# Layernorm, block quantisation and weight loads of an attention and FFN kernel moved to other chunks of a round

## The reference, cut to what matters

```python
xn = layernorm(x)                        # x: 4 sequences x 1024 tokens x 256, over the last axis
q, k, v = split(xn @ w_qkv.T)            # 16 heads of 128; rotary embedding on q and k
attn = softmax(q @ k.T / sqrt(128)) @ v
a = attn @ w_out.T
up_q, down_q = mxfp4(up_kernel), mxfp4(down_kernel)   # blocks of 32: power-of-2 scale, 8-value grid
f = gelu(xn @ up_q + up_bias) @ down_q + down_bias
out = x + a + f
```

## Time and profile before

| | before |
|---|---|
| median of 3 runs | 2655.05 us (2653.35 to 2657.96) |
| the profiled execution | 2657.86 us |
| its span, first to last instruction | 2656.1 us |
| PE busy | 2497.0 us, 94% |
| DVE busy | 2038.3 us, 77% |
| POOL busy | 1826.7 us, 69% |
| ACT busy | 1357.1 us, 51% |
| mean granted TensorE clock | 0.97 |

### The profile page before, as it was taken

How to read it: one execution, slowest core, us unless ns; L and a number is a source line. 1 busy time by engine, 2 the same in 40 slices (tenths; PEclk the granted TensorE clock), 3 DMA queues, 4 the chain that set the end, 5 groups by cost and what they waited for, 6 DMA issues and landing times. The chain is left out here.

```text
span 2656.1 us, 41956 instructions
## 1 busy us (share of the span) xinstructions
PE 2497.0 (94%) x12656; PEld 2166.2 (82%) x12656; DVE 2038.3 (77%) x3209; ACT 1357.1 (51%) x2518; POOL 1826.7 (69%) x1480
## 2 busy tenths in 40 slices
PE   6898999989899898989989898998989899898999
PEld 5787887878788787878878787887878788787788
DVE  6878778687777868787786877878687787868777
ACT  5455554545555454555545455554545555454333
POOL 5678776767777676777767677776768777676321
PEclk8999999999999999999999999999999999999999
DMA  3454545546554554546545454555655455454742
GB/s 100 124 141 115 142 121 129 135 119 171 147 138 124 128 134 121 135 119 171 152 127 135 126 133 116 142 126 132 160 154 129 119 141 129 119 133 114 207 164 64
DMA packets 233732, 354.30 MB, mean 133 GB/s; under 512 B 37840, under 2 KB 95440, under 8 KB 233424
## 3 DMA queue, kind: packets, MB, share of 16 engines
q1 hardware_dynamic: 233680, 353.72, 51.5%
HBM read 66.26 MB, written 18.87 MB: 32 GB/s over the span
## 5 line engine op out<-in xcount | busy, mean ns | idle before, releaser
L915 PE MATMUL o_ps<-keys_first,v_rows 128*128 128x256 f32 x4096 | 946.8, 385 | 4.1 <-DMA keys_first<-turned_blocks 4.1
L589 ACT ACTIVATE probs<-s_ps,neg_max 128x1024 f32<-128x1024 f32 x512 | 571.1, 1115 | 659.9 <-DVE neg_max L688 654.9
L688 DVE TENSOR_REDUCE neg_max<-s_ps 128x1 f32<-128x1024 f32 x512 | 622.2, 1220 | 363.8 <-PE s_ps L915 363.6
L915 PEld LDWEIGHTS o_ps<-keys_first,v_rows 128*128 128x128 f32 x4096 | 779.7, 194 | 109.2 <-DMA keys_first<-turned_blocks 4.5
L915 PE MATMUL s_ps<-seq_parts 128*128 128x512 f32 x3072 | 833.5, 409 | 11.1 <-ACT probs L589 7.1
L466 POOL TENSOR_TENSOR rope_a<-rope_a,cos 128x512 f32<-128x512 f32 x253 | 326.8, 1292 | 611.7 <-ACT rope_b L581 611.5
L915 PEld LDWEIGHTS s_ps<-seq_parts 128*128 128x128 f32 x3072 | 579.0, 189 | 130.5 <-ACT probs L589 7.3
L698 DVE STREAM_TRANSPOSE turned_blocks<-probs 128x512 f32<-128x512 f32 x1024 | 638.2, 679 | 33.3 <-ACT probs L589 14.8
L915 PE MATMUL slot_ps<-seq_parts,w_parts 128*128 128x512 f32 x1500 | 385.8, 392 | 0.0
L595 ACT ACTIVATE o_hi<-o_ps 128x256 fp32r<-128x256 f32 x256 | 98.6, 385 | 535.4 <-PE o_ps L915 535.4
L469 POOL TENSOR_TENSOR seq_parts<-rope_a,rope_b 128x512 fp32r<-128x512 f32 x253 | 327.0, 1293 | 19.8
(11 more groups left out here) (103 smaller groups left out, 2212.9 us busy)
## 6 DMA issues: line engine op xcount, KB each, us to landing
keys_first<-turned_blocks SPq DMA_DIRECT2D x2048, 128.0 KB, 2.7
w_raw<-in_w_qkv SPq DMA_DIRECT2D x96, 256.0 KB, 3.1
seq_parts<-xnt_parts SPq DMA_DIRECT2D x14, 1024.0 KB, 7.6
wo_raw<-in_w_out SPq DMA_DIRECT2D x64, 128.0 KB, 2.5
y<-in_x SPq DMA_DIRECT2D x16, 256.0 KB, 3.2
ln_x<-in_x SPq DMA_DIRECT2D x16, 256.0 KB, 3.5
xnt_parts<-ln_hi SPq DMA_DIRECT2D x16, 256.0 KB, 2.9
xnt_parts<-ln_lo SPq DMA_DIRECT2D x16, 256.0 KB, 3.3
```

The lines of the kernel that those rows point to most:

```text
L589: nc.scalar.activation(probs[:, k2 % 4, :], s_ps[k2 % 2][:, :], ACT.Exp, bias=neg_max[:, col:col + 1], accum_out=row_sum[:, col:col + 1]). ...
L688: nc.vector.tensor_reduce(neg_max[:, k2 % 16:k2 % 16 + 1], s_ps[k2 % 2][:, :], AXX, ALU.max, negate=True).then_inc(max_ready, 1)
L915: ins = nc.tensor.matmul(out, w, m, start=(n == 0), stop=(n == len(terms) - 1))
```

## The change

What a round adds is placed in other steps. `mean` goes from step 1 to step 0; `newton` stays in step 3, `normalise` goes from step 3 to step 4; the layernorm transposes go from (4, 1) to (5, 1), and `ln_lo` with them from step 5 to step 6. The eight parts of the quantisation go from steps 3 (two parts), 4, 5, 6 (two), 7 (two) to steps 0, 5, 6, 7, 8 (two), 9, 11, its transposes from (10, 1) to (13, 1). The value group 0 takes slot (4, 1), which the layernorm had, and in both halves of a round the last "qk0" group takes place 4 in the counting. The stores of both go one and two steps later. ACT's wait on these stores goes from step 15 to step 3. In the last round the quantised weights are loaded in two goes: all of `up_w` and 1792 of the 2048 columns of `down_w` at step 12, the last 256 columns at step 15; before, all of it at step 13. In the prologue v takes the fourth place and the fourth q/k group the fifth.

```diff
-        GROUPS = {(3, 0): (0, "qk0", 0), (3, 1): (1, "qk0", 1), (4, 0): (2, "qk0", 2), (5, 0): (3, "qk0", 3),
-                  (5, 1): (4, "v", 0), (6, 0): (5, "v", 1), (6, 1): (6, "v", 2), (7, 0): (7, "qk1", 0),
+        GROUPS = {(3, 0): (0, "qk0", 0), (3, 1): (1, "qk0", 1), (4, 0): (2, "qk0", 2), (4, 1): (3, "v", 0),
+                  (5, 0): (4, "qk0", 3), (6, 0): (5, "v", 1), (6, 1): (6, "v", 2), (7, 0): (7, "qk1", 0),
...
-        USED = {"qk0": 4, "v": 11, "qk1": 12}
+        USED = {"qk0": 5, "v": 11, "qk1": 12}
-        LN_SLOT, MX_SLOT = (4, 1), (10, 1)
-        MX_PARTS = {3: (0, 1), 4: (2,), 5: (3,), 6: (4, 5), 7: (6, 7)}
+        LN_SLOT, MX_SLOT = (5, 1), (13, 1)
+        MX_PARTS = {0: (0,), 5: (1,), 6: (2,), 7: (3,), 8: (4, 5), 9: (6,), 11: (7,)}
...
-                    if k == 6:
+                    if k == 7:
                         store_ln(r)
...
-                    if k == 12:
+                    if k == 14:
                         store_mx(r)
...
+                    if last_round and k == 12:
+                        sp.wait_ge(mx_stored, (ROUNDS - 1) * 16)
+                        sp.dma_start(up_w[:, :].bitcast(F32), d["mx"][:, 0:MX_HALF]).then_inc(mx_w_loaded[0], 16)
+                        sp.dma_start(down_w[:, 0:MX_HALF - MX_STEP].bitcast(F32),
+                                     d["mx"][:, MX_HALF:MX_COLS - MX_STEP]).then_inc(mx_w_loaded[1], 16)
-                    if last_round and k == 13:
+                    if last_round and k == 15:
                         sp.wait_ge(mx_stored, ROUNDS * 16)
-                        for m in range(2):
...
+                        sp.dma_start(down_w[:, MX_HALF - MX_STEP:].bitcast(F32),
+                                     d["mx"][:, MX_COLS - MX_STEP:]).then_inc(mx_w_loaded[1], 16)
...
+                if k == 3 and not first:
+                    act.wait_ge(ln_stored, i * 32)
+                    act.wait_ge(mx_stored, i * 16)
...
-                if k == 15:
-                    act.wait_ge(ln_stored, (i + 1) * 32)
-                    act.wait_ge(mx_stored, (i + 1) * 16)
...
-                if k == 1:
+                if k == 0:
                     dve.wait_ge(ln_loaded, (i + 1) * 16)
                     mean(i + 2, ln_x, LN_COLS)
                 if k == 3:
                     newton(i + 2, LN_COLS)
+                if k == 4:
                     normalise(i + 2, ln_x, ln_xn, LN_COLS)
```

More of the change, by code:

```diff
@@ L44 @@
 LN_STEP = TILES // ROUNDS
+MX_HALF = MX_COLS // 2
 def layer(nc, d):
@@ L403, in batch @@
                         load_x(0)
-                    if last_round and k == 13:
+                    if last_round and k == 12:
[4 more added lines that the diff above has]
+                    if last_round and k == 15:
                         sp.wait_ge(mx_stored, ROUNDS * 16)
-                        for m in range(2):
-                            cols = slice(m * MX_COLS // 2, (m + 1) * MX_COLS // 2)
-                            dst = (up_w[:, :], down_w)[m]
-                            sp.dma_start(dst.bitcast(F32), d["mx"][:, cols]).then_inc(mx_w_loaded[m], 16)
+                        sp.dma_start(down_w[:, MX_HALF - MX_STEP:].bitcast(F32),
+                                     d["mx"][:, MX_COLS - MX_STEP:]).then_inc(mx_w_loaded[1], 16)
             batch(0, True, False)
@@ L1054, in _ @@
             pe.wait_ge(rope_in, 6)
+            pe.wait_ge(v_ready, 1)
             scores(1, 0, False)
@@ L1090, in slot @@
                     if first and k == 0:
-                        pe.wait_ge(v_ready, n + 1)
+                        if n == 1:
+                            pe.wait_ge(v_ready, 2)
                     else:
@@ L1124, in group @@
                     down(b, n, f)
-            pe.wait_ge(mx_w_loaded[1], 16)
+            pe.wait_ge(mx_w_loaded[1], 32)
             pe.wait_ge(probs_ready, TOK * HEADS // P)
```

## The result

The changed kernel takes 2532.51 us (median of 4 runs, 2529.94 to 2532.98); the kernel before took 2656.51 beside it. The ratio is 0.9533, with a 95% interval of 0.9522 to 0.9544: 124 us less. The forecast was 2512, in a range of 2488 to 2546. The direction and the mechanism were right; 20 us of the forecast gain are missing.

A forecast was written before the change was run, and what follows sets the result against it. PE was taken as the bound, losing 10.47 us a round to waits; less 1.55 of new stalls, 133.8 over fifteen rounds plus 8.9 and 0 made 142.7 off 2657.86, and 2.8 lower for the median: 2512.4 us, range 2488 to 2546.

The forecast's parts named there:

- A free round: PE's work in one round with no waits, unchanged in sum by the change: 144.80 us.
- Fifteen rounds: Gain from step 4 to step 4: 15 times 10.47 us of old loss less 1.55 of new stalls, 133.8 us.
- What follows: Gain behind the fifteen rounds: 8.9 us from the last round's steps 4 and 8, and 0 at the end.
- The end term of 0: Kernel's end: shorter wait behind the weights against moves delayed by the new load, taken as 0, bounds 5 gain and 5 loss.
- Step 6: Stall from quantisation part 1 in step 5's tail, 3.35 to 3.9 us against 3.4 that fit: 0 to 0.5, taken as 0.25.
- the bound of 3.9: Upper price in us of part 1 in step 5's tail, if its first instruction meets a whole POOL one.
- The allowance of 3.4 us: What DVE's tail may hold in a step of 8.7 us, such as step 5, before PE waits.
- Step 9: Stall from step 8's tail, four DVE instructions beside busy POOL, 4.6 us against 4.4: 0.2, bounds 0 and 1.3.
- Step 10: Stall from step 9's late tail, 2.0 + 0.8 us against 1.65 that fit: 1.1, bounds 0 and 2.5.
- Step 11: No stall: lateness ends in step 10's empty tail, and late moves, at most 2.5 us, were taken as harmless.
- every moved instruction meets a whole POOL one: Rival: stalls of 1.3 and 2.5 us from steps 8 and 9, 0.5 from step 5; at most 2556 us; chance 0.20.
- POOL late: Rival: DVE blocks POOL in steps 7 to 9, PE waits about 1.5 us in step 11; 2536 us; chance 0.05.

The follow-up runs named there:

- run 10: Run 9's kernel with the refill of the first q/k weights issued at steps 3 and 11, behind those steps' moves, not at 1 and 9: 2488.70 us.
- run 4: The changed kernel with all quantised FFN weights loaded at step 15 of the last round, without the early load at step 12: 2538.96 us.
- run 8: Run 7's kernel with the FFN's first input loaded at step 10 of the last round, not at 11: 2500.59 us.
- run 7: The changed kernel with part 1 cut in two, its second half and parts 2 to 4 in step 6, part 5 in step 7, part 6 in 8: 2500.49 us.
- Run 1: The changed kernel with the last three instructions of quantisation part 1 moved from step 5's tail to step 6's: 2507.31 us.
- run 6: The kernel before with only the quantisation spread as in the change, its transposes in slot (12, 1) and the layernorm left in place: 2539.02 us.
- run 9: Run 7's kernel with one POOL instruction, the low half of the next pair's first weights, moved behind two rotations: 2561.10 us.

## Why the prediction was right, and where it was off

The bound was right: PE's loss sat in step 4, its cause was the tail ahead of it, and the change takes it away. A free round was put at 144.80 us; run 10 measured 144.83.

The spans go from 2656.1 to 2528.1, 128.0 less, where 142.7 were forecast:
- **Fifteen rounds**: 2329.02 - 2212.11 = 116.9, forecast 133.8. The stalls left are 2.64 us a round (147.47 - 144.83) and not 1.55.
- **What follows**: 2656.1 - 2411.56 = 244.5 before, 236.2 after, 8.4 less; forecast 8.9. The end term of 0 held within 1 us (steps 13 to 15 of the last round take 24.5 us, and 25.5 before), but not quite for the reason given: the wait behind the weights is gone, and the new one, at step 13, is not made by the weights' load (run 4). It follows the input's load (run 8 moves the load, and the stall moves with it), which goes out 1.6 us later against step 12 than before; that this lateness comes from step 9 is argued from the rows of run 7, not shown.
- **Ahead of the rounds**: 2.7 less, forecast 0. In the other kernels with this prologue the same stretch takes 80.0 to 84.7 us, so this is scatter between executions; its cause stays open.

That is 14.7 of the 20 us missing. The other 5.4 lie between one execution and the median: the forecast took the median to be 2.8 us below the profiled execution, as before, and it is 2.6 us above it. That part is scatter between executions.

The four stalls, by the prediction's own terms:
- **Step 6, 0.25 forecast, 1.61 found** (11.42 - 9.81). The step that failed is the price of part 1: 3.35 us, at most 3.9, were taken over from the earlier trace rows, and it took 4.85. Of the difference, 1.02 us are the second instruction, which had slipped in ahead of POOL's next one before, and 0.34 the first (0.66 before, 1.00 here); the bound of 3.9 had thought of the first alone. The allowance of 3.4 us was right: 4.85 + 0.24 - 3.4 = 1.7. A duration was moved to another place without asking what POOL does there, while the same list priced steps 8 and 9 by POOL. Run 1 settles it: 15 x 1.61 = 24 of the 25 us that it wins.
- **Step 9, 0.2 forecast, 0.67 found** (8.96 - 8.29). The tail was 4.92 and not 4.6.
- **Step 10, 1.1 forecast, 0.12 found.** The tail was 0.78 and not 2.0, since step 9's lateness had emptied POOL's queue for a moment. The price was taken from POOL's busy time of before, which the stall itself changes.
- **Step 11, 0 forecast, 1.1 in every fourth round**, 0.22 a round. It is late moves that hold SP's queue, and the next sequence's input behind them. The prediction let late moves go, as only `output` had waited for those of step 4; what else stands behind them on SP was not asked.

1.36 + 0.47 - 0.98 + 0.22 is 1.07 us a round, 16 us of the 16.9 missing.

Of the rivals, "every moved instruction meets a whole POOL one" came true in step 5 alone. "POOL late" named the right place and the wrong reason: it appeared in run 7, when steps 8 to 10 became free, with POOL's 21 instructions as long as ever. On the Trainium skill's rule (SBUF — State Buffer, "Who interferes with whom") of a lock that blocks both ways for whole instructions: DVE's small instructions agree, those of 0.17 us too, which began first. L755 (128x256) does not: before, it began 0.02 us ahead of POOL's next instruction and still took 1.47 us, for 0.41 alone. For POOL the rows show 1.33, 1.47 and 1.48 us beside three 128x256 instructions of DVE, and at most 1.54 (run 7, at 1146.20), against 1.28 alone, and no lengthening beside 128x8 ones. So POOL lost 0.05 to 0.26 us there, less than the 0.41 that DVE's instruction lasts; that it is blocked for a whole one is not seen.

## What to carry to other kernels

Before moving small instructions of DVE, look at POOL's timeline where they will land, not only at their durations where they stand: an instruction of eight columns costs 0.17 us beside an idle POOL and up to 1.2 beside a busy one, unless it slips in between two of POOL's, and one of 128x256 costs 0.41 and up to 1.5. Each pays up to about 1 us, whatever its size, so it is their number that counts. A cheap one may be cheap only where it stands. Spread work to the steps in which POOL idles rather than to the steps with most slack. And when a step is moved later on one engine, follow each semaphore that it raises to the queue that waits on it: a refill behind it on the DMA queue turned a gain of 12 us into a loss of 60.

## What the runs showed of the hardware

- A contending instruction of DVE that begins while POOL is at one ends when POOL's ends, within 0.04 us for 128x8 (1.00, 1.19, 1.22 and 1.10 us) and 0.28 behind it for L775 of 128x256 (1.43).
- A small one that begins in the pause between two of POOL's is not held up: L782, 0.01 us ahead of POOL's next, took 0.17 us before and in run 6; in the changed kernel, begun behind it, the same instruction takes 1.19.
- The reciprocal took 0.20 us beside POOL and alone.
- The clock did not fall after every wait of the same length. In front of the sixteen matmuls with the values, waits of PE of 2.05, 2.52, 2.70 and 2.83 us (run 9, the change, run 10, run 7) were followed by 5.41 us for 3.72, with a granted clock of 0.66 in the change and in run 9; in run 1 waits of 3.19 and 2.32 us in steps 13 and 14 of the last round were followed by 3.72 at 1.00. Why stays open. After waits of up to 1.5 us (step 6) it stayed at 1.00.
